# Third phase of a graph network: three source rows of a block by TensorE and 22 by gather, in place of two and 23, with another order of work

## What is computed

```python
# first layer (two mean aggregations over the edges)
h = x @ W_lin + b_lin
h = tanh(mean_aggregate(h) @ W1_agg + h @ W1_root + b1)
out = tanh(mean_aggregate(h) @ W2_agg + h @ W2_root + b2)
x = layernorm(x + out)
# second layer (an edge network gates the messages)
h = x @ Wn.T + bn
w = ssp(edge_attr_64 @ We1.T + be1)      # ssp(v) = softplus(v) - log 2
w = ssp(w @ We2.T + be2)                 # per edge, 64 values
agg = segment_sum(h[src] * w, dst)
x = layernorm(x + ssp(agg @ Wc.T + bc) @ Wp.T + bp)
```

## Time and profile before

| | |
|---|---|
| median of three runs | 8534.42 us |
| the profiled execution | 8529.04 us, span 8527.1 us |
| TensorE, weight loads busy | 7506.0 us (88%), 6812.9 us (80%) |
| VectorE busy | 4727.1 us (55%) |
| ScalarE busy | 5879.0 us (69%) |
| GpSimd busy | 6267.9 us (74%) |
| third phase, first gather to the start of the last | 4709.0 to 8450.0 us |
| gathers of the third phase | 2875 = 125 x 23 |

### The profile page before, as it was taken

The page is one execution under the profiler, slowest core; times in us unless marked ns, Lnnn a source line. Parts: engine busy times, 40 slices in busy tenths (PEclk is TensorE's granted clock), DMA queues, the critical chain, the costliest instruction groups (busy, mean ns, idle before and its releaser), DMA issues. The chain is left out here.

```text
span 8527.1 us, 164066 instructions
## 1 busy us (share of the span) xinstructions
PE 7506.0 (88%) x46924; PEld 6812.9 (80%) x46925; DVE 4727.1 (55%) x6607; ACT 5879.0 (69%) x10176; POOL 6267.9 (74%) x6471
## 2 busy tenths in 40 slices
PE   7999999999989999999998777777777777777776
PEld 6999999999989999999997666666666666666665
DVE  5555555555455555555556555555555555555555
ACT  5777777777577777777774666666666666666665
POOL 5777777777577777777774777777777777777776
PEclk9999999999899999999997988888888888898988
DMA  2111111111121111111111222222222222222221
GB/s 76 34 34 34 34 34 36 34 34 34 26 44 35 35 34 34 34 34 36 34 34 45 73 56 56 56 56 56 56 57 58 56 56 56 56 56 57 59 56 56
DMA packets 341138, 392.67 MB, mean 46 GB/s; under 512 B 165118, under 2 KB 240562, under 8 KB 340563
## 3 DMA queue, kind: packets, MB, share of 16 engines
q0 software_dynamic: 204000, 151.96, 12.4%
q1 hardware_dynamic: 136750, 239.87, 8.3%
q10 hardware_dynamic: 322, 0.03, 0.0%
HBM read 375.47 MB, written 15.92 MB: 46 GB/s over the span
## 5 line engine op out<-in xcount | busy, mean ns | idle before, releaser
L710 PE MATMUL banks<-split_sb,e_low_hot 128*128 128x400 f32 x22000 | 4136.2, 346 | 46.8 <-DVE split_sb L765 25.2
L710 PEld LDWEIGHTS banks<-split_sb,e_low_hot 128*128 128x128 f32 x22000 | 3977.8, 188 | 95.3 <-DVE split_sb L765 47.2
L940 POOL DMA_INDIRECT big<-hn_table,src_i x2875 | 2860.6, 995 | 890.0 <-issue 859.0
L677 ACT ACTIVATE e_key_off<-e_key_in,node_off 128x384 f16<-128x384 f16 (+1 forms) x4000 | 2028.9, 578 | 129.1 <-DMA e_key_in<-sel_dram 45.0
L656 POOL DMA_INDIRECT big<-p_table,src_i x1750 | 1658.9, 948 | 605.3 <-issue 533.0
L656 POOL DMA_INDIRECT big<-h_table,src_i x1750 | 1676.4, 958 | 541.1 <-issue 532.5
L681 ACT ACTIVATE e_low_hot<-e_key_off 128x1536 fp32r<-128x1536 f16 x1000 | 1381.1, 1381 | 882.1 <-PE banks L710 864.1
L771 DVE TENSOR_REDUCE picked<-banks 128x48 f32<-128x1200 f32 x1000 | 1303.9, 1304 | 1069.1 <-PE banks L710 1053.5
L975 PE MATMUL banks<-hn_split,e_low_hot 128*128 128x448 f32 x7000 | 1594.5, 387 | 76.3 <-issue 69.8
L975 PEld LDWEIGHTS banks<-hn_split,e_low_hot 128*128 128x128 f32 x7000 | 1387.5, 201 | 236.0 <-issue 108.5
L991 PE MATMUL banks<-hot,big 128*64 128x128 f32 x6250 | 563.3, 342 | 768.6 <-DVE hot L1137 768.6
(11 more groups left out here) (216 smaller groups left out, 4522.4 us busy)
## 6 DMA issues: line engine op xcount, KB each, us to landing
e_wide<-in_edge_t SPq DMA_DIRECT2D x125, 832.0 KB, 4.5
e_key_in<-sel_dram SPq DMA_DIRECT2D x250, 343.8 KB
big<-hn_table,src_i POOLq DMA_INDIRECT x2875
big<-p_table,src_i POOLq DMA_INDIRECT x1750
big<-h_table,src_i POOLq DMA_INDIRECT x1750, 2.4
e_key_in<-gate_dram SPq DMA_DIRECT2D x125, 64.0 KB
src_i<-in_src SPq DMA_DIRECT2D x375, 12.5 KB, 1.7
e_key_in<-sel_dram SPq DMA_DIRECT2D x250, 8.2 KB
```

The costliest lines, as they stand in the source:

```text
L677: act.activation(off[:, h, :], key_in[u][:, es], ACT.Abs, bias=node_off[:, h:h + 1])
L710: last = pe.matmul(o, low_hot[gr][:, h, e], split_sb[:, part, h * HI1:(h + 1) * HI1, :], start=(h == 0 and part == 0), stop=(h == HI2 - 1 ...
L940: pool.indirect_dma_start(buf[u][:, j, 0:F], None, table, bass.IndirectOffsetOnAxis(ap=src_i[u][:, j:j + 1], axis=0),).then_inc(gathered[u ...
```

## The change

In the third phase the last three slots are picked by TensorE and 22 are gathered. Three picks with two banks each don't fit into the PSUM left over, so a pick is done in two halves of 14 matmuls, one bank each, that go round banks 0, 1 and 6; `take` multiplies each half apart (448 elements in place of 896) and reduces once. The one-hot row of numbers that was in bank 6 moves into bank 7. The gates are written into the buffer of the second logarithm, so the second logarithms of n+1 wait until the gating of n has read it. Picked slots' tiles that no longer fit (`masked`, `high`, `key_in`) move into a tile of the earlier phases that is free by then (`spare`). The preparation of keys in the first stage handles three slots in place of two. And the order of the step is another:

- VectorE: windows, gating of n, half 0 of n, take slot 0 of n+1, gates of n+1, windows, half 1 of n, take slot 1, first activation of n+2, take slot 2, second values of n+2.
- TensorE: pick slot 0 of n+1, add up half 0 of n, pick slot 1, first layer of n+2, add up half 1 of n, pick slot 2, second layer of n+2.
- ScalarE: second logarithms of n+1, first logarithms of n+2, low_hot of slots 0, 1 and 2 of n+2.

```diff
-GSEL = 2
+GSEL = 3
+HALF_BANK = (0, 1, 6)
...
-            lg1, gate_e, lg2 = (wide[:, k, :] for k in range(2, 5))
-            s1 = lg1
+            lg1, u_e, lg2 = (wide[:, k, :] for k in range(2, 5))
+            s1, gate_e = lg1, lg2
...
-            iota_ps = bank[6][:, 0:WIN]
+            iota_ps = bank[7][:, 2 * WIN:3 * WIN]
...
                     def pick(n, s):
                         pe.wait_ge(low_made, GSEL * n + s + 1)
-                        pe.wait_ge(pick_taken, GSEL * n + s + 1)
-                        for h in range(GLOW):
-                            for part in range(2):
-                                for c in range(2):
-                                    last = pe.matmul(bank[c][:, 0:GHALF * F], low_hot[s][:, h, :],
+                        for c in range(2):
+                            half = 2 * s + c
+                            o = bank[HALF_BANK[half % 3]][:, 0:GHALF * F]
+                            pe.wait_ge(pick_taken, 2 * GSEL * n + half + 1)
+                            for h in range(GLOW):
+                                for part in range(2):
+                                    last = pe.matmul(o, low_hot[s][:, h, :],
...
-                        last.then_inc(pick_psum, 1)
+                            last.then_inc(pick_psum, 1)
...
                     def body(n, g, u):
+                        more = not isinstance(n, int) or n + 2 < NB
                         pick(n + 1, 0)
-                        second_layer(n + 1)
+                        add_up(0, n, u)
                         pick(n + 1, 1)
-                        add_up(0, n, u)
-                        if not isinstance(n, int) or n + 2 < NB:
+                        if more:
                             first_layer(n + 2, turn_of(g, u) + 1, u % 2)
                         add_up(1, n, u)
+                        pick(n + 1, 2)
+                        if more:
+                            second_layer(n + 2)
...
+                            if q == 0 and (not isinstance(n, int) or n > 0):
+                                act.wait_ge(gated, n)
+                            log_of(lg2[:, cs], u_e[:, cs], None, log2_made)
...
-                        dve.wait_ge(pick_psum, GSEL * n + s + 1)
-                        dve.tensor_tensor(masked[:, :, :].rearrange("p f (c a) -> p f c a", c=2), found, mine,
-                                          ALU.mult).then_inc(pick_taken, 1)
+                        for c in range(2):
+                            half = 2 * s + c
+                            found = bank[HALF_BANK[half % 3]][:, 0:GHALF * F].rearrange("p (a f) -> p f a", f=F)
+                            mine = high[:, s, c * GHALF:(c + 1) * GHALF].unsqueeze(1).to_broadcast([P, F, GHALF])
+                            dve.wait_ge(pick_psum, 2 * GSEL * n + half + 1)
+                            dve.tensor_tensor(masked[:, :, c * GHALF:(c + 1) * GHALF], found, mine,
+                                              ALU.mult).then_inc(pick_taken, 1)
...
+                    def body(n, g, u):
+                        ahead = not isinstance(n, int) or n + 1 < NB
+                        more = not isinstance(n, int) or n + 2 < NB
+                        since, to, first = windows(dve, n, 0, True)
+                        gate_messages(n, g, u)
                         half(0, n, since, to, first)
-                        if values_ahead:
-                            take(n + 1, 1, (u + 1) % 2)
+                        if ahead:
+                            take(n + 1, 0, (u + 1) % 2)
+                            gates(n + 1)
                         since, to, first = windows(dve, n, 1, True)
                         half(1, n, since, to, first)
...
+                        if ahead:
+                            take(n + 1, 1, (u + 1) % 2)
                         if more:
                             first_activation(n + 2)
+                        if ahead:
+                            take(n + 1, 2, (u + 1) % 2)
+                        if more:
+                            second_values(n + 2)
```

More of the change, by code:

```diff
@@ L191, in gnn_kernel @@
         acc = sb("acc", [P, ACC])
-        h1_degT = sb("h1_degT", [CQ * (H + 1), NPACK * P])
+        spare = sb("spare", [P, NPACK * P])
+        h1_degT = spare[0:CQ * (H + 1), :]
         inv_deg = sb("inv_deg", [P, NQ])
@@ L277, in gnn_kernel @@
         gate_row = tiles.enter_context(nc.sbuf_tensor("gate_row", [NB, GSEL * P], F16))
-        gate_src_i, gate_p_i, gate_q_i = [
+        gate_src_i, gate_p_i = [
             h1_deg[:, :, :].rearrange("p n c -> p (n c)")[:, k * 2 * GSEL * P:(k + 1) * 2 * GSEL * P]
-            .bitcast(I32).rearrange("p (s c) -> p s c", s=2) for k in range(3)]
+            .bitcast(I32).rearrange("p (s c) -> p s c", s=2) for k in range(2)]
+        gate_q_i = big[:, 1, 0:2 * GSEL * P].bitcast(I32).rearrange("p (s c) -> p s c", s=2)
         digit_i = tiles.enter_context(nc.sbuf_tensor("digit_i", [P, DIGITS, HI2, 32], I32))
@@ L858, in gate_phase @@
             sums = [bank[7][:, h * WIN:(h + 1) * WIN] for h in range(2)]
-            iota_ps = bank[6][:, 0:WIN]
+            iota_ps = bank[7][:, 2 * WIN:3 * WIN]
             took = SLOTS - GSEL
-            key_in = [tiles.enter_context(nc.sbuf_tensor(f"{tag}_key_in{u}", [P, GSEL * P], F16)) for u in range(2)]
             low_hot = [tiles.enter_context(nc.sbuf_tensor(f"{tag}_low_hot{s}", [P, GLOW, P], F32R)) for s in range(GSEL)]
-            high = tiles.enter_context(nc.sbuf_tensor(f"{tag}_high", [P, GSEL, GHIGH], F32))
-            masked = tiles.enter_context(nc.sbuf_tensor(f"{tag}_masked", [P, F, GHIGH], F32))
+            at = [0, F * GHIGH, (F + GSEL) * GHIGH]
+            masked = spare[:, at[0]:at[1]].rearrange("p (f a) -> p f a", a=GHIGH)
+            high = spare[:, at[1]:at[2]].rearrange("p (s a) -> p s a", a=GHIGH)
+            key_in = [spare[:, at[2] + u * GSEL * P // 2:at[2] + (u + 1) * GSEL * P // 2].bitcast(F16) for u in range(2)]
+            assert at[2] + GSEL * P <= NPACK * P
             keys_in = [sem(f"{tag}_keys_in{u}") for u in range(2)]
@@ L1010, in _ @@
                     pick(0, 1)
+                    pick(0, 2)
+                    second_layer(1)
                     with pe.Fori(0, turns) as g:
@@ L1060, in body @@
                     def body(n, g, u):
-                        more = not isinstance(n, int) or n + 2 < NB
-                        if more:
-                            low_hots(n + 2, 0, turn_of(g, u) + 1, u % 2)
                         second_logs(n + 1)
-                        if more:
+                        if not isinstance(n, int) or n + 2 < NB:
                             first_logs(n + 2)
-                            low_hots(n + 2, 1, turn_of(g, u) + 1, u % 2)
+                            for s in range(GSEL):
+                                low_hots(n + 2, s, turn_of(g, u) + 1, u % 2)
                     first_logs(0)
@@ L1072, in _ @@
                     low_hots(0, 1, 1, 0)
+                    low_hots(0, 2, 1, 0)
                     first_logs(1)
-                    low_hots(1, 0, 1, 1)
-                    low_hots(1, 1, 1, 1)
+                    for s in range(GSEL):
+                        low_hots(1, s, 1, 1)
                     with act.Fori(0, turns) as g:
@@ L1088, in _ @@
                     dve.sem_inc(u_made, NG)
-                    dve.sem_inc(pick_taken, 1)
+                    dve.sem_inc(pick_taken, 3)
                     def first_activation(n):
@@ L1119, in take @@
                                               ALU.is_equal)
-                        found = banks[:, 0:1024].rearrange("p (c w) -> p c w", w=512)[:, :, 0:GHALF * F].rearrange(
-                            "p c (a f) -> p f c a", f=F)
-                        mine = high[:, s, :].rearrange("p (c a) -> p c a", c=2).unsqueeze(1).to_broadcast(
-                            [P, F, 2, GHALF])
                         dve.drain()
-                        dve.wait_ge(pick_psum, GSEL * n + s + 1)
-                        dve.tensor_tensor(masked[:, :, :].rearrange("p f (c a) -> p f c a", c=2), found, mine,
-                                          ALU.mult).then_inc(pick_taken, 1)
+                        for c in range(2):
[5 more added lines that the diff above has]
+                                              ALU.mult).then_inc(pick_taken, 1)
                         dve.drain()
@@ L1155, in half, with gate_messages @@
                             dve.tensor_tensor(a_w, a_w, sums[h], ALU.add).then_inc(acc_added[h], 1)
-                    def add_up(n, g, u, values_ahead=True):
-                        since, to, first = windows(dve, n, 0, True)
+                    def gate_messages(n, g, u):
                         dve.wait_ge(gathered[u], 16 * took * (g + 1))
@@ L1191, in _ @@
                     first_activation(1)
+                    take(0, 2, 0)
+                    second_values(1)
                     with dve.Fori(0, turns) as g:
@@ L1194, in _ @@
```

(3 more changed lines are left out.)

16 lines of the change are left out of this document (3 added, 13 removed).

## The result

| | before | after |
|---|---|---|
| median | 8535.39 us (4 runs, 8523.67 to 8537.62) | 8351.9 us (4 runs, 8349.48 to 8352.18) |
| profiled execution | 8529.04 us | 8351.62 us |
| granted TensorE clock, mean | 0.940 | 0.984 |
| third phase, first gather's start to last gather's end | 3742.0 us | 3559.9 us |

What follows compares the result with a forecast made beforehand. The prediction took GpSimd's gathers to bound the third phase: 8529.0 - 155.0 (gathers) - 2.0 (start) + 1.2 (keys) = 8373.2 us, and with half of the median's 5.4 us excess 8376 us, range 8335 to 8430.

Steps and rivals of the forecast that it cites:

- GpSimd sets the phase, one gather is 1.26 us: Third phase: GpSimd's gathers pace it; one gather less takes each block from 29.89 to 28.63 us, 155.0 us over 123 blocks.
- (a): Third phase: gathers slowed beside VectorE's gating and gates keep costing 0.92 us a block, expected within 0.5 of this.
- (b): Start of the third phase: the third block starts about 2 us earlier; its 5.63 us stop may vanish or double.
- (c): Preparation of keys in the first stage: eight longer instructions add between 0 and 2.8 us, taken as 1.2.
- The loop of TensorE and VectorE in 27.7 us: Third phase: one turn through both engines can take 27.7 us, 0.9 us to spare against GpSimd's 28.63 us block.
- Rival 1: Third phase: the loop of TensorE and VectorE becomes the bound; at 29.2 us a block, 8447 us; 15 in 100.
- Rival 2: Third phase: gathers slow down, 0.5 us more lost a block, 8438 us; 8 in 100.
- Rival 3: Third phase: TensorE's granted clock stays at 0.89, its work takes 30.4 us a block, slower at 8592 us; 4 in 100.
- Rival 4: Third phase: nothing moves, since something else paces it at 29.9 us a block, 8530 us; 2 in 100.

Runs made afterwards that it cites:

- the kernel with PSUM inputs: Changed kernel whose gating and gates read one input from PSUM instead of SBUF (wrong messages): 8265.92 us, ratio 0.9682 to the kernel before.
- Two slots in the new order: Changed kernel with two slots picked and 23 gathered, its order, banks and buffers kept: 8519.45 us, ratio 0.9993 to the kernel before.
- the old order: Changed kernel with three picks by halves, but all three engines in the sequence of before: 13,617.1 us, ratio 1.0561, in the other regime only.
- the other regime: First series of seven edited kernels, in which the unedited kernel before took 12,897 and 12,886 us; the changed kernel was not run there.
- the second trace: Trace of the changed kernel run again without edits, as control: 8342.65 us against 8525.01, ratio 0.9785.
- 1.48 us more of TensorE: Changed kernel with 7 more half-bank matmuls ahead of the third slot's pick, products overwritten: 8419.80 us, ratio 0.9861 to the kernel before.
- the split gating: Changed kernel with the gating in two pieces by halves of slots, the second behind half 0's hot tile: 8401.40 us, ratio 0.9857 to the kernel before.

## Why the prediction was right, point by point

- **GpSimd sets the phase, one gather is 1.26 us**: right. 1.26 x 123 = 155.0 of the 177.4, and the kernel with PSUM inputs shows that it is still the pace at 27.74 us. Two slots in the new order show that the gain is the third pick's and not the order's. Whether the old order would have carried three picks is not shown: its only run is in the other regime.
- **Held gathers, (a), "I take the nearest row, 0.92"**: the term that was mis-sized. It measured 0.76 (0.74 in the second trace): 0.16 x 123 = 20 us. The rule that I read off (the gating keeps its lag, the gates move) was right in kind. The lag stayed (median 1.72 and 1.68 us). But I counted the same for late gatings, of which there are fewer, and for gates, of which one instruction a block now meets a gather's start, for 0.15 us a block where it was 0.23.
- **The start, (b), third block 2 us earlier**: 5.7 us from the phase's first gather (64.8 to 59.1), the stop being 1.19 in place of 5.63. 3.7 us more than the term, and luck has a part in the total: 3.7 us of scatter ahead of the phase went the other way.
- **Keys, (c), 1.2 us**: 1.5; the first gather of all starts at 82.94 in place of 81.44 us, and at 82.94 again in the second trace. The rest of the 5.25 us by which that execution starts the phase later (4714.20 against 4708.95) is scatter. With -0.5 of the tail and -1.5 that I don't assign: 5.25 - 5.7 - 155.0 - 20 - 0.5 - 1.5 = -177.4.
- **The loop of TensorE and VectorE in 27.7 us**: right, and near. It measured 27.5, from the first blocks' gatings and again from those of the kernel with PSUM inputs. TensorE has one wait of 1.63 us (1.7 forecast) and none ahead of half 1, second logarithms start at the gating's end, a half multiplication is 0.622 us (0.62). With 1.48 us more of TensorE the round measured 28.96. By the stretch's busy times a block has 19.2 us of VectorE (19.6 forecast) and 21.6 of ScalarE (22 to 22.6).
- **Rival 1** did not come about, but both edits that touch the round (matmuls, a late second piece) made it the bound at once. **Rival 2**: the mean gather is 0.989, not above 1.02. **Rival 3**: the granted clock is 1.00 in the stretch. Between 5000 and 8250 us TensorE's longest wait is 1.8 us, where it was 5.1, and the falls stopped: between the phase's first and last gather it was at 1.2 GHz for 803 us before and 17 after. The rule of the Trainium skill ("TensorE: Matmul & The Clock Gate", A second HAM failure mode: psum-queue depth-cycling) that I set beside it is not borne out here. **Rival 4** falls with the result.
- The Trainium skill ("GPSIMD Engine Reference", Specifications) on contention with VectorE's instructions of two SBUF inputs: the trace agrees, 1.52 us beside the gating with two, 0.96 beside the same with one of them in PSUM.

## What to carry to other kernels

When one engine paces a stage by a fixed step, price a change by its steps and then look for what lengthens them: here the instructions of another engine with two SBUF inputs cost the pace their rest, 0.74 to 0.92 us a block. Lay the round of the other engines out by hand before moving work to them, and count every wait for a buffer in it, the added ones first: the split gating lost 59 us, by the chain of its trace to a wait on a buffer that I had shared. A wait in a round of two engines is not room: TensorE waits 1.63 us a block, of which only the 0.96 between the round's 27.5 and the block's 28.46 was spare, and 1.48 us of new work lengthened the block by 0.50. To measure a round that is not the bound, look for blocks in which it has not caught up yet: two starts of the same instruction there gave 27.5 us.

## What the runs showed that was not expected

- The price of a held gather follows from its start and the other instruction's end alone, and a gather already running is not held (0.96 us). Nor does it hold the other much: in the changed kernel run again, gatings that start beside a running gather take 1.82 to 1.86 us.
- GpSimd's record can hide that a slower round has taken over: 4.1 us of waits in all, while its gathers lost 1.22 us a block.
- Kernels can rank otherwise in the two regimes: two slots have 0.9993 in one and 1.0542 in the other.
